# Summing the heads' expert weights in two halves, and adding the halves inside the transposes

## The reference, cut to what matters

```python
s1 = einsum('bshd,nd->bshn', q1, K1); s2 = einsum('bshd,nd->bshn', q2, K2)   # 32 + 32 key scores per head
v1, i1 = top_k(s1, 10); v2, i2 = top_k(s2, 10)
vals, best = top_k(v1[..., :, None] + v2[..., None, :], 10)                  # 10 of 1024 experts per head
scores = softmax(vals)
h = gelu(einsum('bsd,bshkd->bshk', x, W_down[expert_idx])) * scores
out = einsum('bshk,bshkd->bsd', h, W_up[expert_idx])
```

## Time and profile before

| quantity | value |
|---|---|
| median of 3 timed runs | 1072.67 us (1072.32 to 1073.87) |
| span of the profiled execution, first to last instruction | 1070.5 us |
| time around the span (median less span) | 2.2 us |
| PE busy in the span | 973.2 us, 91% |
| POOL, ACT, DVE busy | 893.0, 874.9, 872.4 us |
| mean granted TensorE clock | 0.974 of 2.4 GHz |

### The profile page before, as it was taken

One profiled execution on the slowest core, in us unless ns is written; L12 is line 12 of the kernel. 1 busy time (PEld: TensorE's weight loads), 2 busy tenths in 40 slices (PEclk: granted clock), 3 DMA queues, 4 the chain that ended last, 5 costly groups with the idle time before them and its releaser, 6 DMA issues.

```text
span 1070.5 us, 35810 instructions
## 1 busy us (share of the span) xinstructions
PE 973.2 (91%) x12440; PEld 763.0 (71%) x12440; DVE 872.4 (82%) x2877; ACT 874.9 (82%) x2123; POOL 893.0 (83%) x935
## 2 busy tenths in 40 slices
PE   6798999999999999999999999999999999999865
PEld 6676777777777777777777777777777777777533
DVE  3567888888888888888888888888889888888773
ACT  4668899888888988888898888889888888988752
POOL 1338888988998898889888888988888898888866
PEclk9989999999999999999999999999999999999875
DMA  6010001111110111111011111001111100110000
GB/s 168 14 23 21 18 17 27 24 27 27 23 19 16 27 24 27 27 24 23 11 26 25 27 26 27 21 11 27 25 27 26 28 20 11 27 25 21 13 13 5
DMA packets 70367, 27.25 MB, mean 25 GB/s; under 512 B 47312, under 2 KB 69936, under 8 KB 70192
## 3 DMA queue, kind: packets, MB, share of 16 engines
q1 hardware_dynamic: 69152, 24.58, 10.5%
q10 hardware_dynamic: 1040, 0.39, 0.1%
HBM read 14.47 MB, written 2.10 MB: 15 GB/s over the span
## 4 chain that ended last, share of the span: by engine, by line
DVE 38%; PE 29%; POOL 13%; issue 13%; ACT 6%; DVEq 1%; DMA 0%; POOLq 0%; ACTq 0%; SPq 0%
DVE mw L1002 10%; POOL wsum L1123 7%; PE psXT L398 7%; POOL p L1063 5%; PE psXT L420 5%; DVE cand L976 5%; DVE top L944 5%; PE psF L592 4%; DVE best L971 4%; DVE best L981 3%; ACT ew L790 3%; PE psXT L422 2%; DVE us L956 2%; DVE q L629 2%; DVE negmax L879 2%
## 5 line engine op out<-in xcount | busy, mean ns | idle before, releaser
L1123 POOL TENSOR_TENSOR wsum<-wsum,mw 128x1024 f32<-128x1024 f32 x192 | 452.8, 2359 | 3.1
L1002 DVE SCALAR_TENSOR_TENSOR mw<-psF,cut,ew 128x1024 f32<-128x1024 f32 x256 | 324.5, 1278 | 47.9 <-ACT ew L790 45.2
L790 ACT ACTIVATE ew<-psF,lnz 128x1024 f32<-128x1024 f32 x256 | 285.5, 1128 | 12.4 <-PE psF L592 9.3
L700 ACT ACTIVATE p<-psXT,negmax 128x128 f32<-128x128 f32 x512 | 184.0, 400 | 3.8 <-DVE negmax L879 3.7
L592 PE MATMUL psF<-sel,usT 128*128 128x512 f16 x512 | 158.5, 392 | 30.3 <-DVE mw L1002 27.7
L379 PE MATMUL psXT<-cT,q 96*128 96x128 f32 x1024 | 142.4, 282 | 14.3 <-ACT p L700 11.0
L379 PEld LDWEIGHTS psXT<-cT,q 96*128 96x128 f32 x1024 | 124.2, 191 | 43.6 <-ACT p L700 25.9
L1063 POOL TENSOR_TENSOR p<-p,rrow 128x512 f32<-128x512 f32 x128 | 130.3, 1037 | 25.9 <-DVE rrow L888 25.9
L700 ACT ACTIVATION_READ_ACCUMULATOR p<-psXT,negmax 128x1 f32 x512 | 123.9, 242 | 0.0
L420 PE MATMUL psXT<-pT,c 128*32 128x384 f32 x768 | 110.7, 501 | 2.0 <-ACT pT L625 2.0
L422 PE MATMUL psXT<-pT,c 128*32 128x128 f32 x768 | 108.5, 278 | 0.0
(11 more groups left out here) (133 smaller groups left out, 2340.5 us busy)
## 6 DMA issues: line engine op xcount, KB each, us to landing
cT<-cT_dram SPq DMA_DIRECT2D x32, 96.0 KB, 2.0
c<-c_dram SPq DMA_DIRECT2D x32, 96.0 KB, 2.1
x<-x_dram SPq DMA_DIRECT2D x32, 64.0 KB, 1.8
xr<-x_dram SPq DMA_DIRECT2D x32, 64.0 KB, 2.0
y_dram<-y SPq DMA_DIRECT2D x32, 64.0 KB, 1.5
wqT<-wqT_dram SPq DMA_DIRECT2D x1, 512.0 KB, 5.1
wo<-wo_dram SPq DMA_DIRECT2D x1, 512.0 KB, 6.3
wdT<-wdT_dram SPq DMA_DIRECT2D x1, 512.0 KB, 3.5
```

Source lines behind the costliest of these rows:

```text
L700: ins = act.activation(p[:, k, i, :], bank[BANK[f"x.s{k}"]][:, i * M:i * M + M], ACT.Exp, bias=negmax[:, k, i:i + 1], accum_out=rowsum[:, ...
L790: done(f"e.x{h}", act.activation(ew[:, h % NEW, :], bank[BANK[f"e.s{h}"]], ACT.Exp, bias=lnz[:, t % 4, h:h + 1]))
L1002: done(f"e.w{h}", dve.scalar_tensor_tensor(out=mw[:, h % NMW, :], in0=bank[BANK[f"e.s{h}"]], scalar=cut[:, t % 4, h:h + 1], in1=ew[:, h % ...
L1123: done(f"e.a{h}", pool.tensor_tensor(wsum[:, t % 2, :], mw[:, 0, :] if h == 1 else wsum[:, t % 2, :], mw[:, h % NMW, :], ALU.add))
```

## The change

POOL adds heads 0 to 3 into one half of a larger `wsum` (`e.a1` to `e.a3`) and heads 4 to 7 into another (`e.a5` to `e.a7`; `e.a5` now adds two `mw` buffers, as `e.a1` does). `e.a4` goes from the program and from `POOL_ORDER`. PE transposes both halves, 16 blocks where it had 8, and the second set adds onto the first in PSUM. `e.gate` and everything behind it read what they read before. The mask of head 0 waits for the earlier tile's `e.a5`, where it waited for `e.a4`.

```diff
-        wsum = sb("wsum", [128, 2, NE])
+        wsum = sb("wsum", [128, 2, 2, NE])
@@ w_turn
-                for c in range(EC):
-                    mm = pe.transpose(bank[BANK["e.wturn"]][:, c * 128:c * 128 + 128],
-                                      wsum[:, t % 2, c * 128:c * 128 + 128], ident[:])
+                for g in range(2):
+                    for c in range(EC):
+                        mm = pe.matmul(bank[BANK["e.wturn"]][:, c * 128:c * 128 + 128],
+                                       wsum[:, t % 2, g, c * 128:c * 128 + 128], ident[:], is_transpose=True, skip_group_check=True,
+                                       start=(g == 0 and c % 4 == 0), stop=(g == 1))
@@ mask
-                        after(dve, f"e.a{h + FH - NMW}", t - 1)
+                        after(dve, f"e.a{max(h + FH - NMW, FH // 2 + 1)}", t - 1)
@@ add_weights
-                def step(t):
-                    if h == 1:
-                        pool.wait_ge(s["e.w0"], t + 1)
+                half, first = h // (FH // 2), h % (FH // 2) == 1
+
+                def step(t):
+                    if first:
+                        pool.wait_ge(s[f"e.w{h - 1}"], t + 1)
                         after(pool, "e.wturn", t - 2)
                     else:
                         pool.wait_ge(s[f"e.a{h - 1}"], t + 1)
                     pool.wait_ge(s[f"e.w{h}"], t + 1)
-                    done(f"e.a{h}", pool.tensor_tensor(wsum[:, t % 2, :],
-                                                       mw[:, 0, :] if h == 1 else wsum[:, t % 2, :],
+                    done(f"e.a{h}", pool.tensor_tensor(wsum[:, t % 2, half, :],
+                                                       mw[:, (h - 1) % NMW, :] if first else wsum[:, t % 2, half, :],
                                                        mw[:, h % NMW, :], ALU.add))
                 return step
             for h in range(1, FH):
-                steps[f"e.a{h}"] = add_weights(h)
+                if h != FH // 2:
+                    steps[f"e.a{h}"] = add_weights(h)
@@ POOL_ORDER
-    "k.norm": 3, "x.norm": 1, "e.a3": 4, "e.a4": 4, "k.inner": 3, "e.a5": 4, "t.norm": 2, "e.a6": 4,
+    "k.norm": 3, "x.norm": 1, "e.a3": 4, "k.inner": 3, "e.a5": 4, "t.norm": 2, "e.a6": 4,
```

## The result

The changed kernel takes 1099.46 us, the median of 4 runs (1097.91 to 1099.58), where the kernel before takes 1073.27 (1072.32 to 1074.52). The ratio is 1.0237, 95% interval 1.0222 to 1.0251: slower by 2.4%. The two medians lie 26.2 us apart. The forecast was 1101.5, the range 1096 to 1108.

A forecast was written before the change was run, and what follows sets the result against it. Bound by a chain through DVE, ACT, POOL's sum and divisions, then PE, with PE tied to POOL. 30 x 0.91 = 27.3 plus 1.5 at the end, 28.8 on 1070.5, plus 2.2 for timing: 1101.5 us; range 1096 to 1108.

The forecast's parts named there:

- The removed sum: On POOL, between e.a3 and k.inner: 75 us less POOL work, worth nothing on the path, leaving only longer idle time.
- The added transposes and where they land: On PE before t.mix: 0.117 us each, 0.93 for eight, delaying e.gate through k.top by 0.91 us a tile.
- The signs named beforehand: New profile: transpose group 2.03 us, DVE's wait before e.gate 1.25, k.top to k.top 0.9 longer, chain through the transposes.
- The branch over `e.gate`, `t.div` and `t.cturn`: From the transposes through DVE and PE to t.csb on ACT: 0.91 us later, deciding over x.p1's 0.93 less at most 0.21.
- The 0.02 us to spare at `t.csb`: On ACT: free at 524.05, after t.cturn's end at 524.03 on PE, so 0.02 us comes off the 0.93 delay.
- The tie between PE and POOL: Before x.p1: t.mix on PE and x.n1 on POOL both end at 522.92, so PE's path is equally late.
- The end: Drained end, last two transpose groups: last group starts 0.6 us later, plus 0.9 for its own eight, +1.5 together.
- Dearer transposes: On PE: an adding transpose runs in two pieces, 1.94 us for eight, about 1132 us; chance 0.06.
- The clock: On PE: each group of 16 runs at the lower clock, 3.7 us for 1.09, about 1151 us; chance 0.02.
- VectorE freed: DVE's masks run faster beside an idler POOL, at most 4.3 us gained, about 1097 us; chance 0.05.
- POOL's time comes through: At e.a1: POOL's backlog sets its start, so the saved 2.36 us a tile counts, about 1030 us; chance 0.02.
- absorbed: Some PE wait between 523 and 531 has room, so the tile keeps its 31 us, about 1073 us; chance 0.05.

The follow-up runs named there:

- Experiment 1: Changed kernel (sums_only) with only the first half transposed, 8 blocks, heads 4 to 7 left out of the output: 1069.66 us against 1073.86, ratio 0.9968.
- experiments 2: Changed kernel with only the first half transposed, run once more for a second profile: 1071.03 us, beside 1071.87 for the kernel before.
- Experiment 5: Kernel before, seven sums kept, with only 4 of the 8 blocks transposed: 1074.43 us against 1073.48, ratio 1.0012.
- experiment 4: Kernel before (turns_half), seven sums kept, with four of the 8 blocks transposed twice: 1088.62 us, ratio 1.0131.
- experiment 3: Kernel before, seven sums kept, with each of the 8 blocks transposed twice, the second time over the first: 1099.38 us, ratio 1.0237.
- experiments 7 to 10: y.m3 behind k.key in the kernel before 1084.28 us, in the changed one 1109.66; y.out before e.hid in the kernel before 1093.57, with both moves 1104.17.
- run 16: Not the name of a run: the text says PE "had just run 16 transposes", a verb and a count, so no change or time belongs to it.

## Why the prediction was right

**The removed sum is worth nothing on the path: right.** Experiment 1 gives 3.4 us of 75, and most of what can be placed of it lies in the drained end. POOL's wait before `e.a1` was predicted at "about 3 us or spread over the steps ahead of it"; it was the second.

**The added transposes and where they land: right, the size a little off.** The step says 0.117 us each, 0.93 for eight, 0.91 after the time to spare. Measured: (1.97 - 1.09) / 8 = 0.110 each, 0.88 for eight, and 0.86 on the tile. The mean over the 8 of before holds the first spacing too, which is longer (0.165 us from the first to the second transpose in the trace of before, 0.109 in the rest); added ones only pay the later spacing. The weight loads' pace of 0.108, which I had as the lower bound, was the better price. The signs named beforehand came out at 1.97 us for the group (2.03 expected), 1.19 for DVE's wait (1.25) and 0.86 for the tile (0.9).

The branch over `e.gate`, `t.div` and `t.cturn` does decide, and not `x.p1`. It decided before the change already, by a few hundredths: the weights of `t.cturn` waited for `t.div` then. PE's weight loads before:

```profile
523.70 0.14 PEld L516 LDWEIGHTS psXT<-ident,actx 128*128 128x128 f32 x1 [0.25 <-DVE actx L922]
```

The 0.02 us to spare at `t.csb` were misread, though. `t.csb` started 0.04 us after `t.cturn` had ended before (524.07 against 524.03), and it does so now (537.02 against 536.98) after an idle time of 0.91. So ACT was waiting for `t.cturn` in both, and that branch had no room. From the group's start to `t.cturn` it was 523.73 - 520.74 = 2.99 us and is 536.68 - 532.82 = 3.86, nearly the whole 0.88 more, and from `t.cturn` to `k.top` 7.12 us pass in both. What the tile fell short by lies ahead of the group: in the median of the ordinary tiles it starts 20.89 us after `k.top` before, and 20.87 in the changed kernel. It is 20.87 in experiments 2 and 5 too, which add no transposes, so the added ones are not the reason. That the 0.02 agreed was luck.

**The tie between PE and POOL: right, but not the whole of it.** Experiment 5 takes four transposes away and gains nothing, experiment 4 adds four and pays for all of them. ACT's input of `t.mix` is a third at the same place, which the step did not name.

**The end: wrong by 2.3 us, and the start moved by 1.** Line 944 (946 in the changed kernel), first and last start of `k.top`'s rows:

```profile
L944 DVE MAX8 top<-psXT x512: 177/181/201, 63.8 to 1030.3; 128x8 f32<-128x32 f32 x171
```
```profile
L946 DVE MAX8 top<-psXT x512: 178/181/201, 64.8 to 1056.7; 128x8 f32<-128x32 f32 x171
```

Between the two starts the change costs 991.9 - 966.5 = 25.4 us, where the sum said 27.3. The first `k.top` is 1.0 later; in the ten profiles of the experiments it comes at 63.8 to 66.4, without order, so I do not count it to the change. From the start of the last `k.top` to the end it is 40.91 us, 0.8 shorter than before, where the sum said +1.5. PE there, the last `e.out` of before first, then the last two groups of work after:

```profile
1064.35 3.75 PE L614 MATMUL psF<-wup,gT 128*128 128x128 f32 x16 [1.41 <-DVE gT L1013]
```
```profile
1088.02 2.29 PE L605 MATMUL psF<-ident,wsum 128*128 128x128 f32 x16 [0.38 <-DVE y L1022]
1091.71 2.02 PE L616 MATMUL psF<-wup,gT 128*128 128x128 f32 x16 [1.41 <-DVE gT L1015]
```

The last group does wait for `e.add`, as the step said, and costs 1.2 us more than the 1.07 of the 8 before, where the sum had 0.9. But it starts 0.25 us earlier after the last `k.top` than before, where the step had it 0.6 later: the group ahead of it took 3.05 us, as the clock rose within it, and not 1.97 + 1.7. And the last `e.out` then takes 2.02 us at a granted clock of 1.00, where the same 16 pieces took 3.75 at 0.50 before, and this gain of 1.7 was in no term. The forecast's 28.8 against 25.6 in the profiles is 1.9 too much for the tiles, 2.3 too much for the end and 1.0 too little for the start, so a part of the closeness is errors that cancel.

**The rivals.** *Dearer transposes*: out, an adding transpose costs 0.110, and experiment 3 gives the same time for overwriting. *The clock*: in 532.80 to 534.80, over the group of 16, the granted clock is 1.00. The Trainium skill (TensorE: Matmul & The Clock Gate, Part 4: PE-mode transpose) has it that the full clock does not engage for transposes; the trace does not agree. *VectorE freed*: the masks take 1270 to 1285 ns, 1268 to 1286 before, with POOL's load down by 8%, and DVE's busy time is 872.3 us, where it was 872.4. *POOL's time comes through* and *absorbed*: out by experiments 1 and 4. The chances of the four rivals that lie outside the range add up to 0.15, not to about 0.13.

What I read too narrowly was the length of PE's stretch: I let it end at `k.top`. For this change it made no difference, since the transposes stand ahead of both ends; for experiments 7 to 10 it decided.

## What to carry to other kernels

Work moved from a busy engine to a busier one is priced by the two places, not by the busy shares: here 75 us of GpSimd time were worth about 3, and 25 us of TensorE time cost all 25, while other TensorE work 8 us earlier in the round was free. Before an engine that the chain of waits does not name is taken for free, see when it would have been ready: where two or three engines end within hundredths of each other, adding costs the full price and taking away gains nothing. In a hand-ordered pipeline such ties stand at many places, and a step that is moved out of one wait falls into the next.

## What the runs showed of the hardware

Transposes of 128x128 float32 blocks that add onto a block in PSUM follow one another after 0.109 to 0.110 us at a granted clock of 1.00, as those that overwrite do, and the first one of a group is followed only after 0.165; at 0.50 they follow after 0.213. In the drained end the same 16 pieces of `e.out` took 2.02 us or 3.75 us, by a granted clock of 1.00 or 0.50; before the first PE had just run 16 transposes in 2.29 us, before the second 8 in 1.07. In the first profile of sums_only it took 2.02 us behind 8 transposes that took 1.97 at the lower clock, and in turns_half 3.68 behind 12 that took 2.79 at the lower clock. What raised the clock in time in some of them was not tried.
